# Causal attention on one core: the order in which the row maxima are given out

## The reference

```python
y = einsum('bse,ef->bsf', layernorm(x), W1) + b1     # 16 heads of 16, q, k, v
w = einsum('bhqd,bhkd->bhqk', q, k) / 4
w = w * mask - 1e10 * (1 - mask)                      # mask: lower triangle
attn = einsum('bhqk,bhkd->bhqd', softmax(w), v)
x = x + einsum('bse,ef->bsf', attn, W2) + b2
```

## Time and profile before

| | |
|---|---|
| median of three runs | 3776.41 us |
| the profiled execution | 3782.0 us, of which the instructions span 3780.3 us |
| TensorE busy | 3176.4 us, 84% |
| VectorE busy | 1747.6 us, 46% |
| ScalarE busy | 1189.4 us, 31% |
| GpSimd busy | 352.9 us, 9% |
| L1351, maxima reduced by VectorE, x576 | 680.4 us, 1220 ns each |
| L1388, exponentials of ScalarE, x576 | 583.1 us, 1023 ns each |
| S and maxima on TensorE (L1208), x2560 | 542.9 us |
| PV on TensorE (L1228), x4608 | 318.0 us |

### The profile page before, as it was taken

The page is one execution under the profiler, slowest core; times in us unless marked ns, Lnnn a source line. Parts: engine busy times, 40 slices in busy tenths (PEclk is TensorE's granted clock), DMA queues, the critical chain, the costliest instruction groups (busy, mean ns, idle before and its releaser), DMA issues. The chain is left out here.

```text
span 3780.3 us, 99336 instructions
## 1 busy us (share of the span) xinstructions
PE 3176.4 (84%) x44860; PEld 1864.3 (49%) x44860; DVE 1747.6 (46%) x3244; ACT 1189.4 (31%) x1486; POOL 352.9 (9%) x334
## 2 busy tenths in 40 slices
PE   1688888888788888879957899999999898997898
PEld 0456565656565666634443444444444444443345
DVE  5334333434333333361074665666666656664302
ACT  0122222222222222232002545554545554553300
POOL 0000000000000000000002111121212121100000
PEclk9788888888788888789957999999999999998896
DMA  5422222222222222126813222222222222312394
GB/s 131 109 68 74 68 74 68 74 71 71 71 71 68 74 68 74 33 92 266 359 15 84 52 52 60 56 56 52 52 53 59 52 60 52 68 19 93 124 419 175
DMA packets 235041, 343.30 MB, mean 91 GB/s; under 512 B 115962, under 2 KB 144452, under 8 KB 218244
## 3 DMA queue, kind: packets, MB, share of 16 engines
q1 hardware_dynamic: 222452, 334.40, 30.9%
q10 hardware_dynamic: 12176, 2.66, 0.5%
HBM read 266.15 MB, written 69.24 MB: 89 GB/s over the span
## 5 line engine op out<-in xcount | busy, mean ns | idle before, releaser
L1351 DVE TENSOR_REDUCE b_tops<-b_slot 128x8 f32<-128x1024 f32 x576 | 680.4, 1220 | 361.5 <-PE b_slot L1208 182.6
L1388 ACT ACTIVATE b_probs<-b_slot 128x1024 f32<-128x1024 f32 x576 | 583.1, 1023 | 551.2 <-PE b_slot L1208 395.5
L711 DVE TENSOR_TENSOR a_probs<-a_scores,a_bias_k 128x512 f32<-128x512 f32 x256 | 176.6, 690 | 554.5 <-PE a_scores L570 318.3
L803 ACT ACTIVATE a_probs<-a_probs 128x512 f32<-128x512 f32 x256 | 161.5, 631 | 589.7 <-DVE a_probs L711 588.6
L1228 PE MATMUL b_outT_ps<-b_probs,b_v 128*17 128x128 f32 (+3 forms) x4608 | 318.0, 384 | 6.2 <-ACT b_probs L1388 5.5
L1208 PE MATMUL b_slot<-b_q_stack,b_k_stack 99*128 99x512 bf16 (+3 forms) x1280 | 275.8, 322 | 43.3 <-DVE b_tops L1351 32.8
L1208 PE MATMUL b_slot<-b_k_stack,b_q_stack 96*128 96x512 bf16 (+3 forms) x1280 | 267.1, 323 | 29.4 <-DVE b_tops L1351 20.6
L1155 POOL TENSOR_SCALAR_AFFINE_SELECT b_probs<-b_probs 128x1024 f32<-128x1024 f32 x128 | 139.8, 1093 | 809.5 <-ACT b_probs L1388 809.5
L1208 PEld LDWEIGHTS b_slot<-b_q_stack,b_k_stack 99*128 99x128 bf16 x1280 | 107.2, 100 | 204.6 <-DVE b_tops L1351 61.9
L1208 PEld LDWEIGHTS b_slot<-b_k_stack,b_q_stack 96*128 96x128 bf16 x1280 | 97.6, 98 | 185.4 <-DVE b_tops L1351 61.6
L1762 PE MATMUL f_ps<-f_w_ring,f_hidT 128*32 128x256 f32 x1024 | 184.0, 381 | 2.1 <-ACT f_hidT L1803 2.1
(11 more groups left out here) (215 smaller groups left out, 4492.1 us busy)
## 6 DMA issues: line engine op xcount, KB each, us to landing
f_w_ring<-in_L_ffn_w_dram SPq DMA_DIRECT2D x128, 1024.0 KB, 10.1
parts_dram<-a_parts SPq DMA_DIRECT2D x96, 256.0 KB
parts_dram<-b_parts SPq DMA_DIRECT2D x96, 256.0 KB
a_k_stack<-parts_dram SPq DMA_DIRECT2D x128, 128.0 KB, 3.0
b_k_stack<-parts_dram SPq DMA_DIRECT2D x64, 256.0 KB, 7.1
a_q_stack<-parts_dram SPq DMA_DIRECT2D x64, 192.0 KB, 3.0
b_q_stack<-parts_dram SPq DMA_DIRECT2D x32, 384.0 KB, 4.6
values_dram<-a_v_stage SPq DMA_DIRECT2D x32, 272.0 KB, 2.6
```

Source lines behind the costliest of these rows:

```text
L711: dve.tensor_tensor(dst[:, :].rearrange("p (t c) -> p t c", c=64), src[:, :].rearrange("p (t c) -> p t c", c=64), bias_k[k][:, HG * g + h, ...
L803: act.activation(dst[:, :], dst[:, :], ACT.Exp).then_inc(probs_ready, 1)
L1351: ins = dve.tensor_reduce(out, src, AX.X, ALU.max)
L1388: act.activation(probs_of(b, g, u, h)[:, :], slot_of(step)[:, :], ACT.Exp).then_inc(taken_act, 1)
```

## The change

The first three maxima units of a group (`LEAD`) are given out in the last three beats of the group two before it, in beats 15, 16 and 17, one per beat. The other 15 follow in beats 0 to 14 of the group before it, one per beat. mred moves from beat 13 to 14, mt and mrow from 15 to 16. In beat 16 mt and mrow come ahead of an early unit of the group after. Before the first group all its units, mred, mt and mrow are issued as before, one list after the other, and then the three early ones of the second group.

```diff
+LEAD = 3
     def maxima(b, g):
-        out = [[] for _ in range(BEATS)]
-        units = beat_units("mx", b, g)
-        for n, step in enumerate(units):
-            out[n * (BEATS - 5) // len(units)].append(step)
-        out[BEATS - 5].append(("mred", b, g))
-        out[BEATS - 3] += [("mt", b, g), ("mrow", b, g)]
-        return out
+        units = [[step] for step in beat_units("mx", b, g)]
+        early, late = units[:LEAD], units[LEAD:] + [[] for _ in range(LEAD)]
+        late[BEATS - LEAD - 1].append(("mred", b, g))
+        late[BEATS - LEAD + 1] += [("mt", b, g), ("mrow", b, g)]
+        return early, late
...
-    for steps in maxima(0, 0):
+    for steps in sum(maxima(0, 0), []) + maxima(0, 1)[0]:
         seq += steps
...
-            tops = maxima(*after) if after[0] < B else [[]] * BEATS
+            tops = maxima(*after)[1] if after[0] < B else [[] for _ in range(BEATS)]
             if ahead[0] < B:
                 seq.append(("stack",) + ahead)
+                for n, steps in enumerate(maxima(*ahead)[0]):
+                    tops[BEATS - LEAD + n] += steps
```

## The result

The changed kernel took 3818.33 us in the median of five runs (3812.44 to 3821.25), beside 3780.99 us (3771.68 to 3789.25) before: the ratio is 1.0118, with a 95% interval of 1.0093 to 1.0143 (the two medians alone give 1.0099). It is slower, as forecast (3798 us, range 3764 to 3824), but by more than I reckoned: 37 us between the medians, where the forecast was 22 us above the median of three runs that it started from and 17 above that of five.

The account below looks back on a forecast made before the run. TensorE, the only engine near full, was taken as the bound; +2 us direct and +20 us clock on the profiled 3782.0 gave 3804, or 3798 us for the median, which lies 5.6 lower; range 3764 to 3824.

Parts of the forecast that it names:

- The rotation: Scores and maxima alternating over three PSUM slots: TensorE's waits of 3.3 us in a second group stay.
- bare beats: Beats with 0.88 us of TensorE's work, said to meet VectorE's 1.21 us reduction still, so TensorE keeps waiting.
- the walk: Beat-by-beat reckoning of a group from unhindered costs: second and fourth groups 41.5 us, third 43.55.
- The wait behind mred: End of second and fourth groups: TensorE stands from 35.07 us until mt at 36.32, then again until 37.57.
- the early reduction: VectorE's reduction of the first early maxima, queued behind mred, ends at 37.45 us and holds the second early maxima's slot.
- the meeting with GpSimd: mred's two-input step on VectorE waits about 1.05 us for GpSimd's second subtraction, in second and fourth groups.
- the wait for the rows: TensorE's 0.32 us idle for the negated maxima's rows before a group's scores, said to go except in first groups.
- The direct sum: Change in time apart from clock loss, added over all groups and the start before the first scores: about +2 us.
- The clock: TensorE's granted clock drops to half behind long waits at group ends; 12 to 13 times of 21, 20 us.
- holes: TensorE's idle stretches around mt: 2.5 us in second and fourth groups, 2.9 in first groups of batches 1 to 7.
- a fall: A stretch of TensorE at half clock, some 3.5 us long, said to cost 1.6 us each.
- Rival (a): At group ends TensorE's idle stretches come but mt breaks them and the clock stays up: 3778 us, chance 0.17.

Follow-up runs that it names:

- e1: Changed kernel with useless matmuls filling TensorE's two waits around mt, and mt's PSUM slot asked for ahead of mred; 3770.36 us, ratio 0.9983 to the kernel before.
- e6: No early maxima; units per beat matched to TensorE's other work by kind of group, mred and mt moved too; 3686.47 us, ratio 0.9768 to the kernel before.
- e3: Changed kernel with its three early maxima in beats 16, 17 and 17, behind mt and mrow; 3778.67 us, ratio 1.0003 to the kernel before.
- e4: Changed kernel with the projections' steps one beat earlier, from beat 4 on; 3779.22 us, ratio 1.0007 to the kernel before.
- e2: Kernel before with 7 and 4 useless matmuls ahead of the two token transposes, in the z wait, batches 1 to 7; 3767.01 us, ratio 0.9977.
- e5: Part of the change alone: maxima one per beat in beats 0 to 14, none early, first three doubled up in beats 0 to 2; 3837.77 us, ratio 1.0183.

## Why the prediction was right in direction and wrong in size

The rotation: right. I said that waits for reductions would stay, since bare beats of 0.88 us still meet 1.21 us of VectorE, and that nothing would be won. Second and fourth groups of e1, at full clock, take 41.3 and 41.4 us where the walk had 41.5 and before 41.6; the third takes 43.4 (walk 43.55). e6 shows the other side: 2.8 us a group were to be had there, by an uneven spread.

The wait behind mred: right, in place and length (mt 36.20 against 36.32, restart 37.53 against 37.57). Its two causes were each shown by taking one away, the early reduction in e3 and the meeting with GpSimd in e4. What the meeting costs was put too high: 1.05 us a group in the forecast's bounds, 0.3 to 0.5 in e4, as the wait for the rows comes back. The two-input step took 0.99 to 1.00 us in 14 of 32 where I had 1.05 of waiting and 0.19 of its own.

The direct sum: a small error. The dense attention, from its first scores to its last, took 1363.8 us before, 1406.7 with the change and 1357.1 in e1. So the direct effect was -7 us. I had about nothing inside this stretch, and +2 with the 1.6 us ahead of the first scores, which can't be seen: the first scores start anywhere between 2045 and 2063 us in the eight traces. Second to fourth groups gave 0.1 to 0.4 us each on average, where I had 0.1; first groups of batches 1 to 6 took no longer, where I had 0.5 more; the very first one gave 1.7 for 0.3.

The clock: this is the step that failed. The prediction took 12 to 13 of 21 holes to bring a fall, at 1.6 us each, 20 us. All 21 did, and one more in the first batch. And a fall was not of one size: in the first groups of batches 1 to 6 and the second groups of batches 0 to 6 (13 of the 22) the clock stayed at half for 6.8 us, not 3.4. I had sized it on one fall of the kernel before; the same trace held one of 6.8 us, in batch 1 (e2). By groups, the changed kernel against e1: 53.5 against 50.8 in the first, 44.4 against 41.3 in the second, 43.1 against 41.4 in the fourth. The whole is 1406.7 - 1357.1 = 50 us where I had 20; the number of falls alone would have made it 35 (22 at 1.6). The price of a single stretch was right (1.7 in the fourth group); the doubled ones cost 3.1 in the second and 2.7 in the first, whose end is also covered in part by the wait for mrow's landing. With the direct term that is -7 + 50 = 43 us in the dense stage, where I had 0 + 20; that the time still fell inside the range is in part luck, as the error of the direct term takes back 7 of the 30 us. The medians differ by 37, the rest of the program varying by a few us from run to run. Rival (a), that mt's tenth of a microsecond keeps the clock up, is refuted.

What stays open is what decides. Counted over batches 0 to 6, and for the longest holes also in the first group of batch 7:

| hole | kernel | holes with a fall |
|---|---|---|
| 1.5 us | changed, first group of batch 0 and third groups | 1 of 8 |
| 1.5 us | e4, first group of batch 0 and second to fourth groups | 5 of 22 |
| 1.8 us | before, at the z steps | 7 of 7 |
| 1.8 us | e3, second and fourth groups | 11 of 14 |
| 1.8 us | e5, second and fourth groups | 14 of 14 |
| 2.3 to 2.6 us | changed, first (but of batch 0), second and fourth groups | 21 of 21 |
| 2.6 us | e4, first groups (but of batch 0) | 5 of 7 |

Holes of 1.8 us and more brought a fall far more often than those of 1.5 us (58 of 63 against 6 of 30), but equal holes in equal places of a group come out differently, in e3 even in all three ways. In the changed kernel the lengths of the groups (53.5, 44.4, 43.3 and 43.1 us) and of the falls repeat in each of batches 1 to 6, so its 13 long falls are one outcome repeated and not 13 draws; the forecast's 12 to 13 of 21 treated them as draws. I take it for the hole's place in time. That fits e3, where the profile shows no other difference ahead of the fall, but no run set that place on purpose.

## What to carry to other kernels

Give a helper engine its work where the bounding engine has long work beside it, not the same amount in every beat: the same instructions took 3818 us in one order and 3686 in another (ratios of 1.0118 and 0.9768 to the kernel before). Watch the end of the dependent chain while doing so: e5, too, spread evenly, and lost most by a chain that ended late. Before moving work on a shared queue, write down what then stands between a chain's end (here mred) and the next engine's restart. If that leaves TensorE about 2 us with next to nothing, count on the matmuls behind it running at half clock, for 3.4 us or twice that, and not just on the wait (32 of 35 holes of 1.8 us here); read the length off every fall in the trace, not off one.

## What was not expected of the hardware

Matmuls that compute nothing made the kernel faster: 30 a batch in the changed kernel took 48 us off it, 11 a batch, in seven batches, took 10 us off the kernel before. A wait of 1.5 us with one small transpose in it was followed by half clock in one group and not in the other (e4), and a bare wait of 1.8 us by 6.8, 3.4 or 0 us of it (e3).

The next was forecast, and is as much worth knowing. GpSimd's 2.13 us subtraction held up a 0.19 us instruction of VectorE on 32 numbers per partition until it had ended, in either of its two passes; the Trainium skill (SBUF — State Buffer, section Who interferes with whom) has this for a VectorE instruction with two SBUF inputs, and the traces agree: 0.99 us beside the subtraction, 0.19 without.
